# A recurrence carried in two rounded parts on 48 rows, with the engines' orders rewritten around it

## The reference

```python
x = x + _L0_attn_a_ref(_layernorm(x), ...)    # gated linear attention, 16 heads, then an MLP with gelu
x = x + _L0_ffn_ref(_layernorm(x), ...)       # 8 experts, the two best by a router, weighted
x = x + _L0_attn_b_ref(_layernorm(x), ...)    # a recurrence with 16 states
x = x + _L0_ffn_ref(_layernorm(x), ...)       # the experts again

def _L0_attn_b_ref(x, A, B, C, W_out, b_out):
    xB = jnp.einsum('bsd,dn->sbn', x, B)
    def step(h, xb_t):
        h = jnp.tanh(xb_t + h @ A.T)
        return (h, h)
    _, hs = jax.lax.scan(step, h0, xB)
    y = jnp.einsum('sbn,nd->bsd', hs, C)
    return y @ W_out.T + b_out
```

## Time and profile before

| | us |
|---|---|
| times of the runs shown | 1913.14, 1916.17, 1927.48 (median 1916.17) |
| span of the profiled execution, from its first to its last instruction | 1923.4 |
| of that, to the first L1245 of the recurrence (fill) | 139.37 |
| 31 rounds from there | 1712.26 |
| behind the last L1245 (drain) | 71.75 |
| one steady round | 55.3 |

### The profile page before, as it was taken

How to read it: one execution, slowest core, us unless ns; L and a number is a source line. 1 busy time by engine, 2 the same in 40 slices (tenths; PEclk the granted TensorE clock), 3 DMA queues, 4 the chain that set the end, 5 groups by cost and what they waited for, 6 DMA issues and landing times.

```text
span 1923.4 us, 47590 instructions
## 1 busy us (share of the span) xinstructions
PE 1801.3 (94%) x16264; PEld 1558.7 (81%) x16264; DVE 1314.5 (68%) x3881; ACT 917.9 (48%) x2535; POOL 1120.8 (58%) x1451
## 2 busy tenths in 40 slices
PE   4588999999999999999999999999999999998987
PEld 3467888888888888888888888888888888887765
DVE  4564667777777777777777777777777777776443
ACT  4444445555554555555445545554555555444321
POOL 4575566766666666556666766566567556654111
PEclk8797999999999999999999999999999999999778
DMA  4110000000000000000000000000000000000000
GB/s 128 34 31 16 23 29 24 22 22 22 22 27 27 26 23 17 27 16 27 27 27 22 24 20 22 21 27 27 27 22 17 27 16 28 23 24 6 3 9 11
DMA packets 71883, 47.79 MB, mean 25 GB/s; under 512 B 37616, under 2 KB 71056, under 8 KB 71696
## 3 DMA queue, kind: packets, MB, share of 16 engines
q1 hardware_dynamic: 70176, 45.28, 7.9%
q10 hardware_dynamic: 1648, 1.72, 0.3%
HBM read 30.21 MB, written 16.78 MB: 24 GB/s over the span
## 4 chain that ended last, share of the span: by engine, by line
PE 72%; POOL 15%; ACT 4%; DVE 4%; issue 3%; DMA 1%; POOLq 0%; SPq 0%; ACTq 0%; DVEq 0%
PE ps L996 52%; PE ps L1013 8%; POOL sx L442 7%; PE ps L1002 3%; PE ps L1021 2%; PE ps L1023 2%; POOL r L356 1%; PE ps L1033 1%; PE ps L1053 1%; POOL osq L438 1%; DVE yT L812 1%; POOL stage L460 1%; PE ps L1058 1%; ACT yT L673 1%; PE ps L1250 1%
## 5 line engine op out<-in xcount | busy, mean ns | idle before, releaser
L996 PE MATMUL ps<-we,yT 128*128 128x512 f32 x3072 | 849.3, 416 | 5.3 <-DVE yT L812 3.6
L996 PEld LDWEIGHTS ps<-we,yT 128*128 128x128 f32 x3072 | 558.2, 194 | 109.2 <-DVE yT L812 10.0
L505 ACT ACTIVATE hs<-ps 16x8 f32<-16x8 f32 x1024 | 177.8, 174 | 841.1 <-PE ps L1013 834.9
L1013 PEld LDWEIGHTS ps<-hs,aT 128*128 128x128 f32 x2048 | 354.8, 196 | 114.9 <-issue 62.5
L1013 PE MATMUL ps<-hs,aT 128*128 128x8 f32 x2048 | 333.2, 237 | 46.9 <-ACT hs L505 45.1
L384 POOL TENSOR_TENSOR part<-part 128x256 f32<-128x256 f32 x64 | 47.4, 741 | 413.3 <-ACT part L523 413.3
L760 DVE SCALAR_TENSOR_TENSOR stage<-ps,coef,stage 128x256 f32<-128x256 f32 x384 | 185.1, 482 | 143.6 <-POOL stage L386 114.9
L442 POOL TENSOR_TENSOR sx<-osq,cst 32x512 f32<-32x512 f32 x128 | 214.0, 1672 | 10.0
L760 DVE SCALAR_TENSOR_TENSOR acc<-ps,coef,acc 128x256 f32<-128x256 f32 x384 | 185.0, 482 | 26.8 <-POOL acc L386 12.6
L407 POOL TENSOR_TENSOR orstd<-omean,mhalf 128x32 f32<-128x32 f32 x32 | 174.0, 5438 | 2.7
L812 DVE TENSOR_TENSOR yT<-ps,yT 128x512 fp32r<-128x512 f32 x64 | 44.0, 691 | 109.8 <-ACT yT L684 64.6
(11 more groups left out here) (174 smaller groups left out, 3478.3 us busy)
## 6 DMA issues: line engine op xcount, KB each, us to landing
xin<-in_x SPq DMA_DIRECT2D x64, 128.0 KB
vrow<-vtok SPq DMA_DIRECT2D x32, 256.0 KB, 2.1
vx<-vrow SPq DMA_DIRECT2D x128, 64.0 KB, 2.0
xag<-in_x SPq DMA_DIRECT2D x64, 128.0 KB
out<-stage SPq DMA_DIRECT2D x64, 128.0 KB
stage<-in_experts SPq DMA_DIRECT2D x1, 2048.0 KB, 8.6
stage<-in_Wvg SPq DMA_DIRECT2D x1, 512.0 KB, 5.0
stage<-in_W SPq DMA_DIRECT2D x1, 512.0 KB, 4.5
```

The lines of the kernel that those rows point to most:

```text
L505: return a.activation(hs[0:N, :, k], bt(ps[0:N, BANK["RB"], 0:TOK])[:, :, k], ACT.Tanh)
L996: ins = t.matmul(dst, left(lp, c), right(rp, c), start=(n == 1), stop=(n == 3 * chunks))
L1013: return t.matmul(bt(ps[0:NP, BANK["RB"], 0:TOK])[:, :, k], aT[:], hs[:, :, (k - 1) % TS], start=False, stop=True, skip_group_check=True)
```

## The change

Six things are changed at once.

1. The state is held on 48 rows, not 16 (NB = 3 * N). A, C and B are each laid down three times. ACT takes tanh twice from the same PSUM column, once rounded to fp32r (h_lead) and once in fp32 (h_whole), and DVE joins them into hs, which is now fp32r: `h_whole * keeps_rest - h_lead`, so that the middle 16 rows hold the rest and the others the negated lead. aT and cw are fp32r too, with lead, lead and rest on the three blocks. So `recur` and the output matmuls are one pass each, and each step has a new station: PE, ACT, ACT, DVE, PE.
2. Bank RB is laid out by step (the 8 batches of a step lie together), which ACT's copy yrT prepares with a permuted write.
3. The attention's tiled matmuls stand in three pieces (all scores and state updates; tile 0; tile 1), before in eight.
4. Three table loads a round: gelu's follows ln's at once, and exp's comes behind gelu.
5. WO and F2 are each cut in two halves by tile, with a `recur` between.
6. The order of all engines is written anew, the loop is cut at another place (PE's body now starts with step 6 of a round and is one stage lower in count), POOL does inner_rstd ahead of sx, and halves nothing for rms_w (DVE does). The weights' start has 13 more small transfers on SP.

```diff
+NB = 3 * N
...
-        bin_, aT = sb("bin_", [P, KC, NP]), sb("aT", [P, NP])
-        cT, woutT, cw = sb("cT", [P, KC, N]), sb("woutT", [P, KC, D]), sb("cw", [N, D])
+        bin_, aT = sb("bin_", [P, KC, NP]), sb("aT", [P, NP], F32R)
+        cT, woutT, cw = sb("cT", [P, KC, NB]), sb("woutT", [P, KC, D]), sb("cw", [P, D], F32R)
...
-        hs = sb("hs", [P, B, TS])
+        hs = sb("hs", [P, B, TS], F32R)
+        h_whole, h_lead = sb("h_whole", [NB, B]), sb("h_lead", [NB, B], F32R)
...
+        late_sync += [(cT[:, :, n * N:(n + 1) * N], wts["C"]) for n in range(3)]
+        late_sync += [(bin_[:, :, n * N:(n + 1) * N], wts["Bin"]) for n in range(3)]
...
+        recurrence_weights = [(a_raw[m * N:(m + 1) * N, n * N:(n + 1) * N], wts["A"]) for m in range(3) for n in range(3)]
...
-            def state_of(k):
-
-                return a.activation(hs[0:N, :, k], bt(ps[0:N, BANK["RB"], 0:TOK])[:, :, k], ACT.Tanh)
+            def state_of(k, count):
+
+                act.wait_ge(sem("rnn_mm"), past((count - 1) * TS + k + 1))
+                a.activation(h_lead[:], ps[0:NB, BANK["RB"], k * B:(k + 1) * B], ACT.Tanh)
+                a.activation(h_whole[:], ps[0:NB, BANK["RB"], k * B:(k + 1) * B], ACT.Tanh).then_inc(sem("rnn_tanh"), 1)
...
+            def split_state(k, count):
+
+                target = value(dve, (count - 1) * TS + k + 1)
+                if k == 0:
+                    dve.wait_ge(sem("RO"), past(count - 1))
+                dve.wait_ge(sem("pads_zero"), 1)
+                dve.wait_ge(sem("rnn_tanh"), target)
+                v.scalar_tensor_tensor(hs[0:NB, :, k], h_whole[:], keeps_rest, h_lead[:].bitcast(F32), ALU.mult, ALU.subtract).then_inc(sem("rnn_h"), 1)
...
-                return t.matmul(bt(ps[0:NP, BANK["RB"], 0:TOK])[:, :, k], aT[:],
+                return t.matmul(ps[0:NP, BANK["RB"], k * B:(k + 1) * B], aT[:],
                                 hs[:, :, (k - 1) % TS], start=False, stop=True, skip_group_check=True)
+
+            def step(k, count):
+
+                if k:
+                    target = value(pe, (count - 1) * TS + k)
+                    pe.wait_ge(sem("pads_zero"), 1)
+                    pe.wait_ge(sem("rnn_h"), target)
+                recur(k).then_inc(sem("rnn_mm"), 1)
...
-                                       hs[0:N, i * BQ:(i + 1) * BQ, :].rearrange("p b t -> p (b t)"), cw[:], start=True, stop=True)
+                                       hs[:, i * BQ:(i + 1) * BQ, :].rearrange("p b t -> p (b t)"), cw[:], start=True, stop=True)
```

More of the change, by code:

```diff
@@ L53 @@
 BANK_ORDER = {
[L54 to L59, removed]
@@ new lines, in body @@
+                if live(it, 2):
+                    for name, count in readers(it, "O"):
+                        pe.wait_ge(sem(name), count)
+                    pe.wait_ge(sem("dec"), c2)
+                    pe.wait_ge(sem("att"), c2)
+                    pe.wait_ge(sem("v_spread"), c2 * 16 * HQ)
+                    attended(0)
+                if live(it, 5):
+                    step(7, c5)
+                if live(it, 4):
+                    for name, count in readers(it, "T1"):
+                        pe.wait_ge(sem(name), count)
+                    pe.wait_ge(sem("ym1"), c4)
+                    transposed(BANK["T1"], m1.y).then_inc(sem("T1"), 1)
@@ new lines, in body @@
+                if live(it, 3):
+                    for name, count in readers(it, "Y1"):
+                        pe.wait_ge(sem(name), count)
+                    pe.wait_ge(sem("y1"), c3)
+                    transposed(BANK["Y1"], y1).then_inc(sem("Y1"), 1)
+                if live(it, 5):
+                    step(9, c5)
+                if live(it, 4):
+                    pe.wait_ge(sem("yT1"), c4)
+                    for name, count in readers(it, "L1"):
+                        pe.wait_ge(sem(name), count)
+                    logits(m1, BANK["L1"]).then_inc(sem("L1"), 1)
@@ new lines, in body @@
+                if live(it, 5):
+                    step(10, c5)
+                if live(it, 4):
+                    for name, count in readers(it, "G1_0"):
+                        pe.wait_ge(sem(name), count)
+                    pe.wait_ge(sem("yT1"), c4)
+                    pe.wait_ge(sem("weights_rest"), REST["experts"])
+                    moe(m1, 0, BANK["G1_0"]).then_inc(sem("moe1"), 1)
+                if live(it, 5):
+                    step(11, c5)
+                if live(it, 4):
+                    for name, count in readers(it, "G1_1"):
+                        pe.wait_ge(sem(name), count)
+                    moe(m1, 1, BANK["G1_1"]).then_inc(sem("moe1"), 1)
@@ new lines, in body @@
+                if live(it, 5):
+                    step(12, c5)
+                if live(it, 2):
+                    attended(1).then_inc(sem("O11"), 1)
+                if live(it, 5):
+                    step(13, c5)
+                if live(it, 4):
+                    for name, count in readers(it, "G1_2"):
+                        pe.wait_ge(sem(name), count)
+                    moe(m1, 2, BANK["G1_2"]).then_inc(sem("moe1"), 1)
+                if live(it, 5):
+                    step(14, c5)
@@ new lines, in body @@
+                if live(it, 5):
+                    step(19, c5)
+                if live(it, 3):
+                    for name, count in readers(it, "F1A"):
+                        pe.wait_ge(sem(name), count)
+                    pe.wait_ge(sem("h2Ts"), c3)
+                    for f in range(0, 2):
+                        ins = product(ps[:, BANK["F1A"], f % 2 * TOK:(f % 2 + 1) * TOK], lambda p, c: wcols(W_1, p, c, FF, f * P, P),
+                                      lambda p, c: h2Ts[:, p, c, :], KC)
@@ new lines, in body @@
+                if live(it, 4):
+                    step(1, c4)
+                if live(it, 3):
+                    for name, count in readers(it, "F2"):
+                        pe.wait_ge(sem(name), count)
+                    pe.wait_ge(sem("gTs"), c3)
+                    product(ps[:, BANK["F2"], 0 * D:1 * D], lambda p, f: gTs[:, p, f, 0 * P:1 * P],
+                                  lambda p, f: wcols(W_2, p, f, D, 0, D), FB)
+                if live(it, 4):
+                    step(2, c4)
```

1031 lines of the change are left out of this document (490 added, 541 removed).

## The result

The changed kernel takes **2055.3 us** (median of 4 runs, 2049.6 to 2060.2) against 1915.5 before: ratio 1.071, interval 1.067 to 1.075. I had forecast 1790. The change makes the kernel slower by 140 us, and the forecast misses it by 265.

The account below looks back on a forecast made before the run. PE's own work was taken to bound the round: 53.95 - 3.6 - 0.8 - 0.4 = 49.1, with 1.9 of waits 51.0 against 55.3; 31 rounds give -133, fill and drain +6, so 1796, as median 1790 us (range 1750 to 1905).

Parts of the forecast that it names:

- part 5: DVE's queue: each split adds 0.09 us (upper end 0.27), DVE has 43.7 a round; PE waits at four places examined.
- rival C: DVE's queue becomes the bound at 0.27 a split, 49.4 us of work; round 58.0, 2006 us; clock might fall; chance 0.12.
- Part 1: Recurrence's matmul, one pass instead of two: one slot of 0.11 us off each of 32 steps, 3.6 a round.
- rival B: The recurrence's removed pass is worth only 0.03 us a step; the round loses 2.6 of the gain; 1870 us; chance 0.12.
- Part 2: The recurrence's output: four fp32 records of 1.06 us become two fp32r matmuls of 0.25, gain 0.8.
- Part 3: Order of tiled matmuls, eight pieces to three: 0.4 us gained for switches that go, between 0 and 0.6.
- Part 4: Recurrence step lengthens from 0.64 to 0.91 us; alone binds only at the two halves of WO, 0.15 a round.
- T1: PE's wait for ym, behind POOL's chain to the shifts: 0.6 us a round, in place of 1.25 now.
- Part 6: ACT and POOL: ACT 29.3 us a round, table loads hidden behind PE, POOL's work stays 35; PE waits 0.6 for ym.
- Part 7: Fill and drain: fill +2 us (-6 to +8), drain +4 (0 to +8).
- D: Stalls from late queues eat the gain: 0.15 us more a step on PE, 4.8 a round; 1920 us; chance 0.08.
- E: Two table loads in a row stall the recurrence at step 21's tanh: +2.4 us a round; 1865 us; chance 0.01.

Follow-up runs that it names:

- e2: Changed kernel with h_whole in PSUM, where the split reads it, and GpSimd waiting for y1 ahead of res, the state's decay and x2b: 1808.4 us, ratio 0.943.
- e9: Changed kernel without the second tanh and the splits (state one rounded value), and with GpSimd's wait for y1: 1712.9 us, ratio 0.894.
- e7: e2 with the fourth table load put back (exp ahead of step 21's tanh, gelu behind step 22's): 1830.4 us.
- e8: e2 with the split of step 13 moved inside the weigh of m1, behind its eighth operation: 1806.7 us.

## Why the prediction was wrong

**The step that failed is part 5**, "DVE's queue": "the 0.09 from one small operation to the next", upper end 0.27. The split was priced by a row of VectorE's operations alone. Which engine worked on SBUF at the same time didn't come into it. Without a collision a split lasts 220 ns and adds (42.95 - 38.31) / 32 = 0.145 us to VectorE's busy time (e2 against e9, 18 steady rounds): between my 0.09 and 0.27. With the collisions it has 356 ns in the mean, above the upper end, and up to 1.27. PE waits for a split 0.87 us ahead of step 16 and 0.62 ahead of step 23, places where I had counted nothing, and 0.55 ahead of step 8. VectorE's 49.1 a round are near C's 49.4, but not for C's reason: in e2 the same queue in the same order with the same 32 meetings has 43.0, against my 43.7, and PE waits for it 0.8 us in a steady round where the changed kernel waits 3.4 (63.8 and 139.2 us in all).

**The second failure is in what I said was untouched.** `y1` stands in part 5 only as work in VectorE's queue; that its own length could change had no term. Before, POOL's x2b, decay and `res` ran ahead of the root that y1 needs (rf, 992.10 in one round); in the changed kernel they stand behind it and so beside y1, which takes 1.85 us longer a round for it: 98 us, from a reordering. I had read the new orders for what waits behind what, not for what runs beside what.

**The third is rival C's last sentence**, where I saw the clock but gave it no price. It is 2.9 of the 9.2 us by which the round (60.2) missed my 51.0.

The terms by themselves:
- Part 1, the pass: 0.11 a step, measured 0.11 (1.61 to 1.50). From start to start the recurrence's matmuls take 5.98 us in a round at a clock of 1.00 before and 2.15 in e9, 0.12 a step. Right, and rival B is out (32 x 0.11 is 3.5 and not 3.6, which changes nothing).
- Part 2, the recurrence's output: I took 1.06 to 0.25. From the first of the two matmuls to the next instruction it is 0.43 in e2. A gain of 0.63, not 0.8; the two here don't go at the rate that I took from twelve in a row.
- Part 3 wasn't tested by itself. From start to start the scores and the attention's matmuls take 3.65 us a round before and 3.04 in e2, 0.6 less: the upper end that I gave, not the 0.4. But it is in the tiled matmuls themselves, not in the switches at `recur` that I counted. Parts 1 to 3 together: 49.1 forecast, 48.8 in e9. That it fits so well is in part luck: the matmuls at L1245 gain 0.28 (0.95 to 0.67), which no part had and no run explains, and the products lose 0.3.
- Part 4, the longer step: 0.91 forecast; the shortest of all steps, in the changed kernel and in e2, is 0.91. Right. But "alone it binds only at the two halves of WO" was too little: see the next.
- The waits of parts 4 to 6 together, 1.95 a round: PE idles only 1.07 in e2, yet the station's share is 2.6 (51.96 - 49.34). The places were mostly right (0.42 behind split 13, 0.2 at step 9), but T1's wait is 0.1 and not 0.6, and one place was missing (0.2 behind split 22); the sum lacked what doesn't show as a wait, 1.7.
- Part 6: the loads. I counted the fourth load's removal as nothing; in e7 it is worth 22 us. And yrT's permuted write, which I had named as unseen, takes 1191 ns (before 573); PE waits for it 0.3 us in all.
- Part 7: fill -1, drain +1 against before in the changed kernel. Forecast +2 and +4.
- The rivals: D and E didn't occur. D's sum was wrong too: 51.0 + 4.8 is 55.8 and not 55.4, about 1938 us and not 1920. C's time (2006) was nearest, by the wrong mechanism.

The sum with the collisions taken out is e2: a round of 51.96 (forecast 51.0), 1808 us (forecast 1790, range 1750 to 1905); 0.7 of the missing 1.0 a round is the station (2.6 against 1.95). Of the 342 us between the changed kernel and e9, 247 are the collisions and the clock behind them, and 96 the station. The pass and the orders gave 202 (1915 to 1713), so the change as written loses by the first of these alone.

It stood in the trace of the kernel before, in two groups of VectorE that I hadn't set side by side: the same shape, both from SBUF.

```profile
L826 DVE TENSOR_TENSOR grel<-gcum 128x256 f32<-128x256 f32 x32 | 42.4, 1325 | 1.1
...
L822 DVE SCALAR_TENSOR_TENSOR glog<-zb,ge 128x256 f32<-128x256 f32 x32 | 13.3, 414 | 2.2 <-ACT ge L571 2.2
```

The first took three times as long because POOL's `res` ran beside it in 27 of 32 rounds; in the changed kernel, moved away, `grel` takes 410. Read with the section "Who interferes with whom" of the Trainium skill ("SBUF — State Buffer"), the pair would have made "1.3 us wherever a split meets POOL" a rival with a price: POOL is busy 35 of 55 us, most of it with such operations, and 32 splits spread over the round must meet it. How many would meet it (10 of 32 in a steady round, 4.5 us of VectorE's time), and how much of that lands on PE, the pair alone didn't tell.

## What to carry to other kernels

When a change puts a small operation on a chain that is waited for, look at what its operands share with the engines that run beside it, not only at its own length. Here VectorE operations with all operands in SBUF wait for the rest of a GpSimd operation that runs (its power apart); for the small one, an operand in PSUM ended that, and for the large one a wait of GpSimd. To find such meetings, compare groups of the same shape in one trace: where the means differ by a factor, print the two engines' timelines over one another and look for ends that fall together.

A wait of PE can cost more than itself: here 2.9 us a round of lower clock came on top of waits of up to 1.9 us, and filling one of them with useless matmuls won 63 us back. A station more in a chain of 32 steps cost 2.6 us a round even when it collided with nothing, so it pays only against a gain above that. And a split moved forward in a full queue (e8) only handed its wait to the next one: look at what then stands ahead of that one.

## What the hardware did that I had not expected

- VectorE against GpSimd on SBUF: exclusion for the rest of the running operation. All 298 long splits end 20 to 40 ns behind GpSimd's end; the y operations that meet it end some 150 ns behind; GpSimd's two-element operation ends 57 ns behind VectorE's.
- GpSimd's power on 128x32 (5.5 us) holds no VectorE operation up: 60 splits within it, none above 230 ns.
- A reordering changed an untouched operation from 406 to 1328 ns, and another (`grel`) from 1325 to 410.
- The granted clock went from 1.00 to 0.50 behind a stretch in which PE worked 1.95 of 4 us, round after round, in a kernel whose PE is busy 90% of a steady round. In e2 it fell behind small tiled matmuls that kept PE busy 3.93 of 4 us.
- In e2 the next piece often starts 0.03 us behind the recurrence's matmul (L1098 behind L1115), elsewhere 0.10 to 0.13; before it was 0.11 behind the second record of the pair.
